# An expert layer that adds its weighted rows by accumulating scatters, with four shared tiles behind the routed ones

## Chip, cores and metric

One core of one Trainium2 chip runs the kernel. The metric is device time in microseconds (us), the median of several runs. The profile is of one more execution of the program, recorded by the hardware profiler.

## What is computed

Eight sequences of 512 tokens by 512 features go through attention with rotary embedding, then through a second block: RMS norm, latent attention with a residual, RMS norm again and a mixture of experts, whose result is normalized and added to the first attention's output. The change lies in the mixture. Each token gets the shared expert and its two best of seven routed experts, weighted by their scores:

```python
shared = expert_ffn(x, sh_gate, sh_up, sh_down)
probs = jax.nn.sigmoid(x @ router_w + router_b)
scores, idx = jax.lax.top_k(probs, TOPK)            # TOPK = 2
scores = scores / jnp.sum(scores, axis=-1, keepdims=True)
w = jnp.sum(jax.nn.one_hot(idx, NR) * scores[..., None], axis=-2)   # NR = 7
for e in range(NR):
    combined = combined + w[..., e:e + 1] * expert_ffn(x, r_gate[e], r_up[e], r_down[e])
return shared + combined
```

with `expert_ffn(x, wg, wu, wd) = (silu(x @ wg) * (x @ wu) / 8) @ wd` and a hidden width of 256. The kernel adds the block's own input `h` to this sum, applies a layer norm to the result, and adds the first attention's output `x1`. That is its output.

## The kernel before, in words

`attention_layers` makes, sequence by sequence, `x1` and `h` and stores them in HBM (`store_h`, L465 to L469), with an order of steps written by a planner. Beside it ScalarE's queue clears the slots for routed rows with `clear` (L678).

`expert_layer` (L1103) works in units of 512 tokens, which `unit(u)` walks through on each engine. Units 0 to 7 are the eight sequences with the shared expert's weights; units 8 to 29 are 22 tiles of routed rows, with the weights of one routed expert each, read from a table. A unit on TensorE (L1923) is four products of 12 matmuls into the ring `into` (gate and up for two halves of the hidden width, banks for gate and up in turn) and two down products of 12 into `down`. Each float32 product is three matmuls of rounded high and low parts. ScalarE takes the tanh and the high parts, VectorE the gating and the low parts (`gate`, `full_acts`, `low_acts`). Weights are loaded by SyncE (SP) into `raw` and split into `wh` and `wl` (`split`).

Between the products stands the opening of a later unit: four columns of transposes (`transposed_rows`) whose high and low parts go to `xh` and `xl`, and for a sequence also its squares, scale and norm (`squares`, `row_scale`, `normed`), its logits, their transposes, the choice of two experts (`routing`), a rank count on TensorE (`rank`, L1909: one product and ten of 7 columns) and the slot numbers (`placing`). Unit u opens sequence u + 2 and places sequence u + 1; two openings come ahead of unit 0. All these use the two banks of the ring `opening` in turn. Then GpSimd scatters the normed rows of the sequence to their two slots in HBM, eight indirect DMAs of 128 rows (`scatter`, L1416). SP loads sequence s into the place of sequence s - 4 in `xr` only when that one is scattered (`load_x`, L1275). When all eight are placed, `make_table` gives the experts and places of the 22 tiles, and SP loads the tiles from the slots (`load_rows`).

The shared result is added to `h` in `hsum` by VectorE (`add_shared`) and stored as `summed`. The routed results are copied to `y` by ScalarE (`take_y`) and stored as `y_slots`. Behind the last unit comes a loop over the eight sequences: SP loads `x1` and `summed` (`load_back`), GpSimd gathers both rows of each token by the numbers that `answers` made (`bring`, L1425: eight indirect DMAs), VectorE adds them weighted by `share` (`gather_rows`), takes statistics, and after `close_scale` on GpSimd normalizes and adds `x1` (`close`), and SP stores. Two sequences are in hand at a time:

```python
for s in range(blocks):
    store(s)
    if s + 2 < blocks:
        load_back(s + 2)
```

Every engine runs its own list in order, and semaphores tie the lists together.

## Time and profile before

| | us |
|---|---|
| median of 3 runs | 2620.97 (2616.71 to 2624.66) |
| profiled execution | 2623.76 |
| its span | 2622.0 |
| busy: TensorE | 2222.6 (85%) |
| VectorE | 1542.5 (59%) |
| ScalarE | 1043.9 (40%) |
| GpSimd | 991.2 (38%) |

In the rows below, PE is TensorE (PEld its weight loads), DVE VectorE, ACT ScalarE, POOL GpSimd and SP SyncE; a q behind a name is that engine's queue, which issues DMAs and waits. PEclk is TensorE's granted clock as a share of the full one, DMA the busy share of the core's 16 DMA engines. Times are from the span's start. L1868 is the line of the helper that issues nearly all products, so groups are told apart by the tiles that they write and read.

### The profile page before, as it was taken

The numbers are of one execution on the slowest core, as the hardware profiler recorded it, in microseconds if no ns is written. First come the engines' busy times: TensorE is split into PE (matmuls) and PEld (weight loads), VectorE is DVE, ScalarE is ACT, GpSimd is POOL, SyncE is SP. The second block draws the span as 40 slices with busy tenths as digits, with TensorE's granted clock in tenths as the row PEclk, the third lists the DMA queues.
The fourth block names the chain that finished last, engine by engine and source line by source line (L and its number), as shares of the span: only waits on it lengthen the run. The fifth ranks groups of instructions, "written<-read, shape, count | busy, mean of one in ns | idle before, by whom it ended". The sixth has DMA issues, their size and how long they took to land. (4 is left out here: it accounts for less than half of the span.)

```text
span 2622.0 us, 38025 instructions
## 1 busy us (share of the span) xinstructions
PE 2222.6 (85%) x12992; PEld 1523.9 (58%) x12992; DVE 1542.5 (59%) x4168; ACT 1043.9 (40%) x2164; POOL 991.2 (38%) x1049
## 2 busy tenths in 40 slices
PE   6898888999888999988899989895899899999700
PEld 5665555665555566554565655552677688888500
DVE  3656656656566565656656566663555555565377
ACT  1335443334444333445433444542332355555300
POOL 1445544435454344536343454542343000000174
PEclk9999989999999999999999999996899899999955
DMA  5334454444445354353553434443354555555397
GB/s 174 97 97 128 123 160 123 113 115 120 129 119 148 109 142 113 98 153 97 155 144 100 131 101 116 109 115 124 127 213 164 209 199 195 207 187 212 145 325 255
DMA packets 228430, 386.11 MB, mean 147 GB/s; under 512 B 24718, under 2 KB 108558, under 8 KB 222606
## 3 DMA queue, kind: packets, MB, share of 16 engines
q1 hardware_dynamic: 157710, 290.87, 37.2%
q10 hardware_dynamic: 60288, 59.25, 7.0%
q0 software_dynamic: 10240, 33.56, 3.5%
q8 instruction: 105, 1.72, 0.3%
q14 instruction: 87, 0.71, 0.1%
HBM read 141.90 MB, written 140.51 MB: 108 GB/s over the span
## 5 line engine op out<-in xcount | busy, mean ns | idle before, releaser
L819 DVE CUSTOM_DVE_ANT_0 unused<-score,mask 128x128 bf16<-128x128 f32 (+3 forms) x1024 | 467.8, 486 | 337.9 <-PE score L1000 324.9
L638 ACT ACTIVATE probs<-scoresT 128x512 f32<-128x512 f32 (+3 forms) x1024 | 418.2, 436 | 610.3 <-PE scoresT L1023 606.3
L1000 PE MATMUL score<-stacks 96*128 96x256 f32 (+2 forms) x1024 | 394.9, 429 | 96.8 <-DMA stacks<-parts 61.7
L1023 PE MATMUL scoresT<-stacks 97*128 97x256 f32 (+2 forms) x1024 | 408.8, 434 | 17.8 <-ACT probs L638 10.7
L571 POOL TENSOR_TENSOR probs<-probs 128x1536 f32<-128x1536 f32 (+1 forms) x128 | 373.8, 2920 | 52.4 <-PE out_ps L1037 45.7
L1000 PEld LDWEIGHTS score<-stacks 96*128 96x128 f32 x1024 | 183.1, 195 | 308.7 <-issue 183.5
L560 POOL TENSOR_SCALAR_AFFINE_SELECT probs<-probs 128x512 f32<-128x512 f32 x256 | 164.3, 642 | 349.4 <-ACT probs L638 349.2
L832 DVE RECIPROCAL total<-total 128x128 f32<-128x128 f32 x256 | 232.6, 932 | 94.9 <-ACT whole L649 89.5
L930 PE MATMUL middle<-wqkv,XT 128*128 128x128 f32 x2048 | 270.1, 280 | 7.0 <-ACT XT L605 6.1
L930 PEld LDWEIGHTS middle<-wqkv,XT 128*128 128x128 f32 x2048 | 260.4, 195 | 21.9 <-issue 8.4
L1058 PE MATMUL middle<-wo,outT 128*128 128x512 f32 x512 | 261.5, 606 | 0.0
L1023 PEld LDWEIGHTS scoresT<-stacks 97*128 97x128 f32 x1024 | 190.2, 195 | 117.3 <-ACT probs L638 68.5
L1431 POOL DMA_INDIRECT wh<-y_slots,answer x32 | 48.3, 1511 | 450.0 <-DMA y_slots<-y 441.2
L1037 PE MATMUL out_ps<-probs,V 128*32 128x512 f32 (+3 forms) x2048 | 205.0, 474 | 4.2 <-POOL probs L560 3.7
L1868 PE MATMUL into<-xh,wh 128*128 128x512 f32 x480 | 198.2, 413 | 0.0
L1868 PE MATMUL into<-xl,wh 128*128 128x512 f32 x480 | 190.2, 396 | 0.0
L1868 PE MATMUL into<-xh,wl 128*128 128x512 f32 x480 | 190.2, 396 | 0.0
L550 POOL TENSOR_TENSOR qk<-qk,turned 128x512 f32<-128x512 f32 x64 | 81.3, 1270 | 270.2 <-DVE turned L763 270.2
L759 DVE TENSOR_TENSOR qk<-middle,rope 128x512 f32<-128x512 f32 (+1 forms) x128 | 70.8, 553 | 126.8 <-PE middle L930 80.6
L1748 DVE SCALAR_TENSOR_TENSOR acts<-acts,into 128x512 f32<-128x512 f32 x60 | 41.2, 687 | 168.0 <-ACT acts L1514 166.0
L801 DVE TENSOR_TENSOR parts<-middle,parts 128x512 fp32r<-128x512 f32 x128 | 84.9, 685 | 80.0 <-ACT parts L614 78.0
L981 PE MATMUL middle<-wqkv,XT 128*128 128x512 f32 x256 | 129.2, 597 | 0.0
(174 smaller groups left out, 3732.6 us busy)
## 6 DMA issues: line engine op xcount, KB each, us to landing
stacks<-parts SPq DMA_DIRECT2D x768, 128.0 KB, 2.8
x_slots<-mask ACTq DMA_DIRECT2D x56, 1024.0 KB, 6.8
xr<-x_slots SPq DMA_DIRECT2D x22, 1024.0 KB, 6.1
y_slots<-y SPq DMA_DIRECT2D x22, 1024.0 KB, 4.3
raw<-in_gates SPq DMA_DIRECT2D x23, 512.0 KB, 3.9
raw<-in_ups SPq DMA_DIRECT2D x23, 512.0 KB, 4.9
raw<-in_downs SPq DMA_DIRECT2D x23, 512.0 KB, 5.7
normed<-in_L_attn_x SPq DMA_DIRECT2D x8, 1024.0 KB, 7.9
```

The lines of the kernel that those rows point to most:

```text
L560: pool.affine_select(out=diagonal, in_=diagonal, compare_op=ALU.is_ge, fill=0.0, base=0, pattern=[[0, GH], [1, P]], channel_multiplier=-1)\
L571: pool.tensor_tensor(probs[0][:, :, P * j:T], probs[0][:, :, P * j:T], probs[j][:, :, :], ALU.add)\
L638: act.activation(probs[j][:, h, 0:width], scoresT[:, u % ST_BANKS, first:first + width], ACT.Exp, scale=SCALE).then_inc(exp_done, 1)
L819: ins = dve.tensor_tensor_reduce(unused[:, t, 0:width], score.bank(name)[:, first:first + width], mask[:, T - width:T], 1.0, MASKED, ALU.a ...
L832: dve.reciprocal(total[:, mine], total[:, mine]).then_inc(inverted, 1)
L930: ins = pe.matmul(to, tile_of(xT, c, t), wqkv[:, c, first:first + P], start=(c == 0), stop=(c == CT - 1))
L981: ins = pe.matmul(middle.bank(name), tile_of(xT, c, t), wqkv[:, c, 2 * D:3 * D], start=(c == 0), stop=(c == CT - 1))
L1000: ins = pe.matmul(score.bank(name)[:, first:first + width], heads[0:ROWMAX, 0, h, t * P:(t + 1) * P], heads[0:ROWMAX, 1, h, 0:width], star ...
L1023: pe.matmul(scoresT[:, u % ST_BANKS, 0:T - first], heads[0:ROWMAX + 1, 1, h, j * P:(j + 1) * P], heads[0:ROWMAX + 1, 0, h, first:T], start ...
L1037: ins = pe.matmul(out_ps[h * HD:(h + 1) * HD, P * j:T], v[:, c % 2, j, head:head + HD], probs[j][:, h, :], start=(j == 0), stop=(j == TT - 1))
L1058: ins = pe.matmul(middle.bank(name), tile_of(outT, (NG * f + c) % OUTS, t), wo[:, core_of(f)[1], c, :], start=(c == 0), stop=(c == CT - 1))
L1868: ins = pe.matmul(to, left, right, start=(first and n == 0), stop=(last and n == len(pairs) - 1))
```

## The change

The expert layer is written anew around one list of steps, `expert_order`, from which every engine takes its own.

- There are 30 units as before: four shared sequences (0 to 3, "early"), the 22 routed tiles, and the four other shared sequences (4 to 7, "late").
- All eight sequences are opened in the first three units, in the order 0, 4, 1, 5, 2, 6, 7, 3. Only sequence 0's columns come ahead of unit 0. The late ones' normed rows are stored (`normed_kept`) and loaded and transposed again for their units.
- A row scattered to a slot carries four numbers more (`ROW = D + 4`): the smaller share, the difference of the shares, the first expert and the token's number. From them `goals` makes each routed tile's weights (`gain`) and target rows (`goal`). ScalarE applies the weight when it copies the down product out.
- `summed` gets the early sequences with their shared result and the late ones as plain `h`, stored by the attention layers. GpSimd adds each routed tile to it by four accumulating indirect DMAs (`give`). Each waits for the landing of the one before, since two additions to a row at once would lose one. Rows of empty slots go to rows that nobody reads.
- Gone are `y_slots`, `answers`, the gathers (`bring`) and `gather_rows`.
- The closings (`close_stats`, `close_scale`, `close_norm` on ScalarE now, `close`) stand in the order 4, 0, 5, 1, 6, 2, 7, 3: two each in the last three late units, one ahead of the down products and one behind them, and two behind the last unit. A late sequence's closing adds its down product. The loads of `summed` (`load_sums`) wait for the last three tiles' additions.
- `rank` counts with one product of 35 columns and four of 28, 21, 14 and 7.

The core of the diff:

```diff
+                    if s >= EARLY:
+                        sp.dma_start(summed[s * T:(s + 1) * T, :].rearrange("(t p) c -> p t c", p=P), rows[:, :, :])\
+                          .then_inc(h_stored, 16)
...
-                    CLEAR = T - 2 * P
+                    CLEAR = TT * ROW // 6
...
+ROW = D + 4
+EARLY = 4
+GIVEN = 3
+SUMS = 2 + GIVEN
...
+                def rows_free(o):
+
+                    b = o - XR
+                    if b >= 0:
+                        sp.wait_ge(*opening.full(("xT", b, CT - 1)))
+                    if 0 <= b < blocks:
+                        sp.wait_ge(scattered[b], 16 * TOP * TT)
+                        if sequences[b] >= EARLY:
+                            sp.wait_ge(xn_kept[sequences[b] - EARLY], 16)
+                    if blocks <= b < blocks + routed:
+                        sp.wait_ge(goal_done, b - blocks + 1)
...
+                def give(k):
+
+                    if k == 0:
+                        pool.wait_ge(h_kept, 16 * EARLY)
+                    pool.wait_ge(goal_done, k + 1)
+                    for t in range(TT):
+
+                        if t > 0:
+                            pool.wait_ge(y_given[k % GIVEN], 16 * (TT * (k // GIVEN) + t))
+                        elif k > 0:
+                            pool.wait_ge(*given(k - 1))
+                        pool.wait_ge(y_done, TT * k + t + 1)
+                        pool.indirect_dma_start(
+                            out=summed, out_offset=bass.IndirectOffsetOnAxis(ap=goal[:, k % XR, t:t + 1], axis=0),
+                            in_=y[:, k % GIVEN, t, :], in_offset=None, compute_op=ALU.add).then_inc(y_given[k % GIVEN], 16)
...
+                def load_sums(m):
+                    s = closing[m]
+                    if m == 0:
+                        sp.wait_ge(h_kept, 16 * EARLY)
+                        for k in range(routed - GIVEN, routed):
+                            sp.wait_ge(*given(k))
+                    if m >= SUMS:
+                        sp.wait_ge(out_ready, TT * (m - SUMS + 1))
...
+                def goals(k):
+
+                    beside = xr[:, (blocks + k) % XR, :, D:ROW]
+                    dve.wait_ge(x_in[(blocks + k) % XR], 16 * ((blocks + k) // XR + 1))
+                    if k >= XR:
+                        dve.wait_ge(*given(k - XR))
+                    if k > 0:
+                        dve.wait_ge(goal_done, k)
+                    dve.scalar_tensor_tensor(out=gain[:, k % XR, :], in0=beside[:, :, 2], scalar=expert[:, k:k + 1],
+                                             in1=beside[:, :, 1], op0=ALU.is_equal, op1=ALU.mult).then_inc(goal_step, 1)
...
+                        if m == 0 and u > 0:
+                            pe.wait_ge(*evacuated(u - 1, t))
...
+        if late > 0:
+            yield from closing_of(2 * late - 2)
+        yield "DN", u, 0
+        yield "DN", u, 1
+        if late > 0:
+            yield from closing_of(2 * late - 1)
+    for m in range(2 * (blocks - EARLY) - 2, blocks):
+        yield from closing_of(m)
```

How the lists change at three places. In these rows a name ahead of `<-` is what the instruction writes, and what stands in brackets is the semaphores that it waits for.

First, VectorE between the gate and up products of unit 0 and its end. L1589 (L1816 in the changed kernel) are squares of a sequence, L1644 (L1877) begins the placing of one, and L1606 (L1836) the routing of one. Before, unit 0's end:

```order
L1748 SCALAR_TENSOR_TENSOR acts<-acts,into 128x512 [waits tanh_done]
L1595 SCALAR_TENSOR_TENSOR xl<-opening,ln2w,xh 128x512 [waits x_high]
L1755 SCALAR_TENSOR_TENSOR acts<-acts,into 128x512 [waits into_filled,into_freed0]
L1761 TENSOR_TENSOR actl<-acts,acth 128x512 [waits act_high]
L1595 SCALAR_TENSOR_TENSOR xl<-opening,ln2w,xh 128x512 [waits x_high]
L1644 TENSOR_TENSOR place<-opening,offset 128x28 [waits opening_filled]
```

and in the changed kernel:

```order
L1980 TENSOR_TENSOR actl<-acts,acth 128x512 [waits act_high]
L1823 SCALAR_TENSOR_TENSOR xl<-opening,ln2w,xh 128x512 [waits x_high]
L1816 ISA junk,square<-xr 128x512 [waits squared,padded2_done,x_in0]
L1816 ISA square 128x1
L1816 ISA junk,square<-xr 128x512
L1816 ISA square 128x1
L1816 ISA junk,square<-xr 128x512
L1816 ISA square 128x1
L1816 ISA junk,square<-xr 128x512
L1816 ISA square 128x1
L1877 TENSOR_TENSOR place<-opening,offset 128x28 [waits opening_filled]
```

The squares of the fifth opened sequence, which wait for its load into the first one's place (`x_in0`), now stand ahead of the placing of the second, and behind that the routing of the third.

Second, GpSimd from the last sequences to the routed tiles. Before, the last two scatters and the first gathers:

```order
L1421 DMA x_slots<-xr,slot 28672x512 [waits placed]
L1421 DMA x_slots<-xr,slot 28672x512 x7
L1421 DMA x_slots<-xr,slot 28672x512 [waits placed]
L1421 DMA x_slots<-xr,slot 28672x512 x7
L1431 DMA wh<-y_slots,answer 128x512 [waits y_kept1,y_kept0,answered]
L1431 DMA wh<-y_slots,answer 128x512 x3
```

and in the changed kernel:

```order
L1639 DMA x_slots<-xr,slot 28672x516 [waits placed]
L1639 DMA x_slots<-xr,slot 28672x516 x7
L1655 DMA h_summed<-y,goal 4224x512 [waits y_done,goal_done,h_kept]
L1655 DMA h_summed<-y,goal 4224x512 [waits y_done,y_given0] x3
L1655 DMA h_summed<-y,goal 4224x512 [waits y_done,y_given0,goal_done]
L1655 DMA h_summed<-y,goal 4224x512 [waits y_done,y_given1] x3
```

The gathers are gone, and each of the four additions of a tile waits for the one before (`y_given`).

Third, VectorE and a sequence's closing. Before, one turn of the last loop:

```order
L1817 SCALAR_TENSOR_TENSOR hsum<-wh,share,hsum 128x512 [waits back_in0_0,h_in0]
L1817 SCALAR_TENSOR_TENSOR hsum<-wh,share,hsum 128x512 x3
L1817 SCALAR_TENSOR_TENSOR hsum<-wl,share,hsum 128x512 [waits gained,back_in0_1]
L1817 SCALAR_TENSOR_TENSOR hsum<-wl,share,hsum 128x512 [waits gained] x3
L1824 BN_STATS stats<-hsum 128x6 [waits gained] x4
L1827 BN_AGGR meanvar<-stats 128x2 [waits stats2_done] x4
L1833 TENSOR_SCALAR hsum<-hsum,meanvar,rstd 128x512 [waits rstd2_done]
L1833 TENSOR_SCALAR hsum<-hsum,meanvar,rstd 128x512 x3
L1838 TENSOR_TENSOR y<-hsum,y 128x512 [waits closed,x1_in0]
L1838 TENSOR_TENSOR y<-hsum,y 128x512 [waits closed] x3
```

and in the changed kernel, the third late unit from its last low part on:

```order
L1823 SCALAR_TENSOR_TENSOR xl<-opening,ln2w,xh 128x512 [waits x_high]
L1999 TENSOR_TENSOR y<-down,y 128x512 [waits down_filled,back_in2]
L1999 TENSOR_TENSOR y<-down,y 128x512 [waits down_filled] x3
L2006 BN_STATS stats<-y 128x6 [waits meanvar2_done,late_added] x4
L2011 BN_AGGR meanvar<-stats 128x2 [waits shift2_done,stats2_done] x4
L2018 TENSOR_TENSOR xr<-hsum,xr 128x512 [waits closed,x1_in1]
L2018 TENSOR_TENSOR xr<-hsum,xr 128x512 [waits closed] x3
L2006 BN_STATS stats<-y 128x6 [waits meanvar2_done,back_in3]
L2006 BN_STATS stats<-y 128x6 [waits meanvar2_done] x3
L2011 BN_AGGR meanvar<-stats 128x2 [waits shift2_done,stats2_done] x4
L2018 TENSOR_TENSOR xr<-y,xr 128x512 [waits closed,x1_in2]
L2018 TENSOR_TENSOR xr<-y,xr 128x512 [waits closed] x3
```

Two closings stand between the gating of one late unit and that of the next. The weighted adds of gathered rows and the normalization are no longer on VectorE.

## Rows read from the trace of the kernel before

**Rows 1.** Busy time of each engine by stage; columns as in the first row, in us.

```profile
core 0: us, PE busy (x) PEld busy (x) DVE busy (x) ACT busy (x) POOL busy (x), PEclk, DMA share, GB/s
0.00:1814.00 1814.00, 1602.76 (x10048) 1030.83 (x10048) 1088.88 (x3202) 744.74 (x1649) 824.59 (x874) 0.96 0.43 121
1814.00:1862.00 48.00, 20.70 (x87) 12.13 (x87) 19.11 (x59) 17.58 (x31) 6.17 (x21) 0.59 0.47 165
1862.00:2073.00 211.00, 198.05 (x964) 155.00 (x964) 113.50 (x358) 60.30 (x103) 69.36 (x74) 0.94 0.55 195
2073.00:2474.00 401.00, 401.00 (x1897) 325.94 (x1896) 222.03 (x358) 220.68 (x382) 0.00 (x0) 1.00 0.52 186
2474.00:2622.00 148.00, 0.07 (x1) 0.00 (x0) 98.95 (x192) 0.60 (x2) 91.07 (x80) 0.51 0.82 291
```

**Rows 2.** Chain of waits, 2474 to 2622 (start, duration, what).

```profile
2520.85 6.37 DMA out<-y
...
2527.64 11.10 DMA hsum<-h_summed
```

**Rows 3.** Chain of waits, routed stage: the down products of two tiles in a row.

```profile
2303.44 5.59 PE down L1868 x24
...
2321.97 5.59 PE down L1868 x24
```

**Rows 4.** Timeline, shared stage: a rank count; the first tanh of two units in a row.

```profile
1875.36 2.48 PE L1919 MATMUL opening<-either,ones 128*128 128x7 f32 x20
...
1941.46 0.60 ACT L1514 ACTIVATE acts<-into 128x512 f32<-128x512 f32 x1
...
1965.90 0.60 ACT L1514 ACTIVATE acts<-into 128x512 f32<-128x512 f32 x1
```

**Rows 5.** Who waited for whom, TensorE, 1862 to 2475.

```profile
PE opening L1885 <- DMA xr<-x_slots: 12.8, 1, 12.8
```

**Rows 6.** DMA issues: queue, count, size, median us to landing.

```profile
xr<-h_kept SPq DMA_DIRECT2D x8, 1024.0 KB, 6.3
...
out<-y SPq DMA_DIRECT2D x8, 1024.0 KB, 5.0
...
x_slots<-xr,slot POOLq DMA_INDIRECT x64, 2.7
```

**Rows 7.** Timeline, start of the expert layer.

```profile
1814.84 0.38 SPq L1281 DMA_DIRECT2D xr<-h_kept  x1
...
1835.23 0.59 PE L1868 MATMUL opening<-xh,wrh 128*7 128x512 f32 x1 [1.77 <-DVE xl L1595]
...
1842.58 3.70 DVE L1579 TENSOR_TENSOR wl<-raw,wh 128x512 fp32r<-128x512 f32 x6 [5.17 <-ACT wh L1470]
...
1861.98 0.48 PE L1868 MATMUL into<-xh,wh 128*128 128x512 f32 x1
```

**Rows 8.** Busy time in the last 17.3 us of the shared stage, behind the hole.

```profile
2050.90:2068.20 17.30, 17.30 (x75) 13.89 (x74) 11.84 (x19) 7.40 (x13) 0.00 (x0) 0.88 0.33 113
```

**Rows 9.** Timeline, last sequence: slot numbers, last scatter's issue, load of the first tiles.

```profile
2027.87 0.17 DVE L1664 CAST slot<-slotf 128x8 uint32<-128x8 f32 x1
...
2037.22 0.96 POOL L1421 DMA_INDIRECT x_slots<-xr,slot  x1 [0.30 <-issue]
...
2044.84 1.51 SPq L1310 DMA_DIRECT2D xr<-x_slots  x2
```

**Rows 10.** DMA issues, 2028 to 2045.

```profile
x_slots<-xr,slot POOLq DMA_INDIRECT x8, 6.1
```

**Rows 11.** Groups of instructions, 1862 to 2474 (count, busy us, mean ns, idle before).

```profile
L1768 DVE TENSOR_TENSOR hsum<-down,hsum 128x512 f32<-128x512 f32 x32 | 21.6, 691 | 40.0 <-PE down L1868 39.8
```

**Rows 12.** Groups of instructions, 2474 to 2622.

```profile
L1838 DVE TENSOR_TENSOR y<-hsum,y 128x512 f32<-128x512 f32 x32 | 19.9, 683 | 0.0
...
L1824 DVE BATCH_NORM_STATS2 stats<-hsum 128x6 f32<-128x512 f32 x32 | 19.7, 679 | 0.0
...
L1442 POOL TENSOR_TENSOR rstd<-padded,minus_half 128x4 f32<-128x4 f32 x8 | 8.3, 1044 | 0.7
```

More of the change, by code:

```diff
@@ new lines, in _ @@
+                for step, *which in order:
+                    if step == "LX":
+                        load_x(*which)
+                    if step == "LS":
+                        load_small()
+                    if step == "LW":
+                        load_weights(*which)
+                    if step == "LH":
+                        load_h(*which)
+                    if step == "LR":
+                        load_tile(blocks + which[0])
+                    if step == "XT" and which[1] == CT - 1 and which[0] < blocks and sequences[which[0]] >= EARLY:
+                        keep_normed(which[0])
+                    if step == "OUT" and units.kinds[which[0]][0] == "early":
+                        keep_h(units.kinds[which[0]][1])
+                    if step == "LSM":
+                        load_sums(*which)
+                    if step == "LX1":
+                        load_x1(*which)
+                    if step == "ST":
+                        store(*which)
@@ L1376, in _ @@
+                for n in range(XR):
+                    sp.wait_ge(stored[n], 16 * (blocks // XR))
             @block.gpsimd
@@ L1446, in _ @@
[L1446 to L1461 removed]
+                                out=flat_slots, out_offset=bass.IndirectOffsetOnAxis(ap=slot[:, o, j, t:t + 1], axis=0),
@@ L1463, in _ @@
+                pool.wait_ge(consts, N_POOL)
+                for step, *which in order:
+                    if step == "SQ":
+                        row_scale(*which)
+                    if step == "RK":
+                        scatter(*which)
+                    if step == "OUT" and units.kinds[which[0]][0] == "routed":
+                        give(units.kinds[which[0]][1])
+                    if step == "CA":
+                        close_scale(*which)
             @block.scalar
@@ L1466, in split @@
                 def split(i, k):
+                    if k == 0:
+                        act.wait_ge(raw_in, 48 * (i + 1))
+                    if k == 0 and i >= 2:
+                        last = max(u for u in range(len(units)) if units.weights(u) == i - 2)
+                        act.wait_ge(*down.full((last, TT - 1)))
                     n, half_of = divmod(k, 2)
@@ new lines, in columns_free @@
+                def columns_free(o):
+                    u = units.unit_of.get(o)
+                    if u is not None and u >= 2:
+                        act.wait_ge(*into.full(("up", u - 2, FT - 1)))
+                        if u - 2 < EARLY:
+                            act.wait_ge(*opening.full(("z", units.opening[u - 2])))
+                    if u is None:
+                        earlier = [b for b in range(o) if b not in units.unit_of]
+                        if earlier:
+                            act.wait_ge(*opening.full(("z", earlier[-1])))
@@ L1963, in _ @@
-                pe.wait_ge(consts, N_POOL)
-                for s in range(2):
-                    for c in range(CT):
-                        transposed_rows(s, c)
-                    logits(s)
-                    logits_by_token(s)
-                rank(0)
-                for u in range(units):
-                    unit(u)
+                        pe.wait_ge(*opening.out(("xT", o, CT - 1)))
+                        pe.wait_ge(*opening.out(("xT", o, CT - 2)))
+                    name = ("gate", "up")[n], u, m
@@ new lines, in into_hidden, with out_of_hidden @@
+                    pairs = []
+                    for c in range(CT):
+                        first = c * FF + m * P
+                        pairs += three((wh, xh), (wl, xl), np.s_[:, i % 2, n, first:first + P],
+                                       np.s_[:, units.home(o), c, :])
+                    pe.wait_ge(*into.empty(name))
+                    product(into.bank(name), pairs).then_inc(into.filled, 1)
+                def out_of_hidden(u, m):
+                    i = units.weights(u)
+                    pe.wait_ge(act_low, u * FT + m + 1)
+                    for t in range(TT):
+                        if m == 0 and u > 0:
+                            pe.wait_ge(*evacuated(u - 1, t))
+                        ins = product(down.bank((u, t)),
+                                      three((acth, wh), (actl, wl), np.s_[:, m, t * P:(t + 1) * P],
+                                            np.s_[:, i % 2, 2, m * D:(m + 1) * D]),
+                                      first=(m == 0), last=(m == FT - 1))
+                        if m == FT - 1:
+                            ins.then_inc(down.filled, 1)
@@ new lines, in _ @@
+                pe.wait_ge(consts, N_POOL)
+                for step, *which in order:
+                    if step == "XT":
+                        transposed_rows(*which)
+                    if step == "LG":
+                        logits(*which)
+                    if step == "ZT":
+                        logits_by_token(*which)
+                    if step == "RK":
+                        rank(*which)
+                    if step == "GU":
+                        into_hidden(*which)
+                    if step == "DN":
+                        out_of_hidden(*which)
```

901 lines of the change are left out of this document (465 added, 436 removed).

## Prediction

> **What bounds the kernel now.** I read the busy time by stage first [rows 1]. The attention layers take 1814 us, and the change touches them only at two edges. The expert layer then has four stages: 48 us before the first gate product, 211 us with TensorE busy for 198 (the eight shared tiles, with routing beside them), 401 us with TensorE busy for all of it at clock 1.00 (21 of the 22 routed tiles), and 148 us in which TensorE does nothing. Next the chain of waits of that last stage [rows 2]: it runs through loads of a summed sequence, 11.1 us each, and stores of 6.4 us. Eight sequences are fetched back, gathered, normalized and stored by VectorE and the DMA engines alone. In the routed stage the chain is TensorE without a break: 18.53 us from one tile's down products to the next one's [rows 3]. In the shared stage a unit takes 24.4 us [rows 4], since it also opens one sequence. There is one hole in it: 12.8 us [rows 5], in which the first routed tile is awaited. So the idle 148 us is the prize, and whatever the change puts into the first two stages or behind the routed ones is its price.
>
> The sum is made against the profiled execution: span 2622.0 us and time 2623.76, while the median of the runs is 2620.97. It therefore ends with +1.8 for what lies around the span and -2.8 to the median, together -1.
>
> **Edge of the layers: +2.7.** Four sequences are stored twice, the last two stores of 1 MB together at the end of the layer, where nothing hides them. 1 MB is 3.6 us at the last stage's mean of 291 GB/s [rows 1], and less where nothing else moves; the bounds are 0 (they overlap) and 5 (a whole out store [rows 6]). I take 2.7. The other three lie beside 50 us of attention without a wait for them. The cleared slots grow by 1/128, hidden in the same way.
>
> **Start of the expert layer: -21.5.** Before, both openings (with logits) come ahead of the first product: 47.1 us from the first load to it [rows 7]. Now only sequence 0's columns do. They are in at 1835.2; then VectorE has the next sequence's squares (2.5) and six weight splits (3.7), so the products start near 1840.5. Bounds -18 and -23.
>
> **The early units: -34.** Before, eight shared units take 206.2 us, from the first gate product [rows 7] to 2068.2, where the first routed tile's begins [rows 8]. Now four units carry all eight openings. TensorE's work: a unit's four gate and up products and its down product are 18.53 less 1.4 for four columns of transposes, 17.1; an opening is 1.4 of columns, 2.8 of logits, 0.35 of their transposes and a rank count, which falls from 20 small passes (2.5 us [rows 4]) to 8, about 1.25 with the product ahead of it. 4 x 17.1 + 8 x 1.4 + 8 x 4.4 is 115. I then followed the queues. Three things stop TensorE:
> - A slot of rows is loaded anew only when its sequence has been scattered. From the slot numbers to the last of eight scatters' issue are 9.3 us [rows 9], then 2.7 to landing and 6.3 for the load [rows 6]: 18 us. VectorE asks for those rows with some 14 us of work in between, and waits before the placing and routing on which TensorE's next ranks and zT transposes hang. That is 4 to 6 us in each of units 0 to 2.
> - Logits, tanh, routing and rank of one sequence now follow each other with one product between instead of a unit, and use two banks in turn: 2 to 5 us in each unit more. By my walk units 0 to 2 take 42, 34 and 45, of which 23 is waiting.
> - Three sequences are opened in unit 2. The last two scatters run one behind the other: 16 x 1.26 = 20 us of issue instead of 10, and landings beside the weight load. Before, 16.9 us go by from the last slot numbers to the load [rows 9]; now about 21 from the last ones. The hole grows from 12.8 to 21.
> 115 + 23 + 21 is 159, plus some 13 for TensorE at its lower clock after such stops (the granted clock was 0.94 in this stage [rows 1], 0.88 after the hole [rows 8]): 172. Minus 206 is -34. Bounds: with half the waits -55; with twice those of units 0 to 2 -10.
>
> **The routed units: 0, with one unknown.** The answer table, the y stores and the 64 gathers go. Four tiny goal operations per tile on VectorE, which is busy 222 of 401 us, are free. The new work is the accumulating scatter: four per tile on GpSimd, each waiting for the landing of the one before. No row shows one. Below, it is bounded by the plain scatter in a quiet fabric, 2.7 us from issue to landing [rows 6]; above, by the same scatter beside a weight load and a store, 6.1 [rows 10]. It must read what it adds to, but runs alone in its queue, and only the weight and row loads (2.5 MB, some 7 of 18.5 us) meet it; so I take 4.3, nearer the quiet row. A tile then costs 4 x 4.4 = 17.6 us, under 18.53: hidden. The cover is thin. If a tile costs G, the last addition ends 22 x G behind the first one's start, which is 21 units (389 us) ahead of the first late unit. The loads of summed rows, which wait for it, can start some 27 us into that unit and still be in when VectorE asks for them in the second. So the penalty is 22 x G - 415 us where positive; it starts at 4.6 us an addition with 0.1 between.
>
> By the Trainium skill, Collectives: The Full Stack, section "The bandwidth ceiling: the fold count and why AG ≠ RS ≠ AR", an add in the DMA engines is slow "because the add needs **two source reads**", and moves at half the rate of a copy. If only the data's part of a scatter doubled (an estimated 0.7 us, a quarter MB at nearly 400 GB/s), an addition would be an estimated 3.4 us and the sum would stay as it is; if the rule held for the whole time, it is the second rival.
>
> **The late units: +88.8.** Four shared units come behind the routed ones: the first undisturbed, 18.5. From the second on VectorE has per unit its own 7 us, and two closings: one add of the down product (4 x 0.69 [rows 11]), two statistics (4 x 0.61), aggregates, two additions of the attention's output (4 x 0.63 [rows 12]): 13.4. That is 20.4 against TensorE's 18.5, and the next unit's tanh stands on ScalarE behind both normalizations, whose scales GpSimd makes in about 2 us (1.04 for the power [rows 12]). TensorE waits for the gate bank and for the add. My walk gives 21.7, 23.5 and 25.1.
>
> **The end: -119.** Before, 147.9 us from the last product to the end. Now five of the eight closings are behind VectorE or in its hands when the last product ends; left are the final addition of one and two whole closings, 5.6 + 2.5 + 2.9 + 2.5 in a row, 2 + 2.6 for the last scales and normalization, the last additions and a store of 5.0 [rows 6]: 29.
>
> **The sum:** 2.7 - 21.5 - 34 + 88.8 - 119 = -83. 2622 - 83 = 2539; I add 6 for additions that now and then miss the cover, and with -1 the median is about **2545**.
>
> **Rivals.**
> - *The early units lose little*: the loads are in on time and banks free early. For it, the shared stage now has only its one hole. Against it, the 18 us of scatter and reload, each part of which has a row. It gives 2545 - 22 = 2523.
> - *An addition takes twice a plain scatter in all*: 5.4 and 0.1 between, G = 22, penalty 69. For it, the added read of the target; against it, that a quiet scatter's 2.7 is largely not data. 2539 + 69 - 1 = 2607. A middle case at 5.0 (G 20.4, penalty 34) gives 2572.
> - *The additions become the bound, and it ends slower*: each takes 6.1 as in [rows 10], G = 24.8, penalty 131, 2669. It decides from 5.6 us an addition (G = 22.7). For it, the weight and row loads that share the fabric; against it, that those eight scatters were issued back to back and queued among themselves, while here one at a time is under way.
> - *The change does not overlap what it says*: the closings wait for the last addition in any case, and then only VectorE's order counts; a tail of 60 instead of 29 would give 2576. It falls into the middle case.
>
> **How the numbers follow.** The forecast has 0.50, the first rival 0.08, the middle case 0.20, doubled additions 0.07, the slower one 0.12, and 0.03 is for a result near no change. The range runs from 2508 to 2605: it holds the forecast, the first rival and most of the middle case, and leaves out the bound additions and half of the doubled ones. A measurement of this kernel tells 0.3% (8 us) from no change. Faster by more: 0.50 + 0.08 + 0.20 + 0.06 = 0.84. Within: 0.03. Slower: 0.13.
>
> **What would show it.** The time from the first expert load to the first gate product near 26 us; units 0 to 2 over 30 us each, with VectorE waiting for a load of rows ahead of a placing; one wait for the first routed tile near 21 us; routed units still at 18.53 with GpSimd waiting for an addition's landing most of the time, 4 to 4.7 us from issue to landing; late units of 21 to 25 us; under 35 us behind the last product. I am wrong if the routed units are longer than 18.6, if GpSimd is still adding when the second late unit starts, or if the early units take over 195 us.

## The result: 2.2% slower, the additions became the bound

| | us |
|---|---|
| before, median of 4 runs | 2619.8 (2616.7 to 2624.7) |
| changed, median of 4 runs | 2679.4 (2673.5 to 2683.3) |
| ratio | 1.022, 95% interval 1.0197 to 1.0246 |
| forecast | 2545 (2508 to 2605) |

The forecast was wrong in sign and size. The result lies near the slower rival's 2669. The profiled execution has a span of 2671.3 us, 49.3 over that of before.

The busy time of each engine by stage, cut at the changed kernel's own borders; it answers to [rows 1]. The stages are attention; the start of the expert layer; four shared units; 22 routed units; four late units; the end:

```profile
core 0: us, PE busy (x) PEld busy (x) DVE busy (x) ACT busy (x) POOL busy (x), PEclk, DMA share, GB/s
0.00:1809.00 1809.00, 1601.14 (x10048) 1031.04 (x10048) 1089.63 (x3202) 746.16 (x1649) 824.60 (x874) 0.96 0.44 124
1809.00:1835.00 26.00, 4.07 (x17) 3.16 (x18) 12.00 (x28) 10.23 (x18) 5.82 (x22) 0.50 0.86 304
1835.00:2013.00 178.00, 132.37 (x625) 97.46 (x626) 94.85 (x382) 53.99 (x96) 70.95 (x76) 0.87 0.54 193
2013.00:2508.00 495.00, 434.69 (x1938) 349.61 (x1937) 241.58 (x438) 225.43 (x392) 119.74 (x75) 0.94 0.61 163
2508.00:2641.00 133.00, 83.19 (x336) 65.70 (x335) 52.48 (x100) 31.15 (x49) 31.76 (x33) 0.79 0.61 169
2641.00:2671.00 30.00, 0.45 (x2) 0.01 (x1) 23.06 (x48) 11.22 (x16) 10.65 (x12) 0.55 0.60 210
```

The routed stage had TensorE busy without a break before. Now it is 495 us long for 435 us of products, and the late units take 133 us for 83. Who waited for whom there: first TensorE and ScalarE in the routed stage (2013 to 2508), then TensorE in the late units (2510 to 2642). Columns: who, for what, us in total, times, longest.

```profile
PE into L2060 <- DVE acts L1967: 56.6, 13, 6.9
PE into L2060 <- DVE acts L1974: 3.7, 1, 3.7
...
ACT y L1751 <- DMA h_summed<-y,goal: 144.5, 13, 13.7
...
PE down L2060 <- DVE hsum L1999: 36.2, 1, 36.2
```

ScalarE scales a tile's down product into one of three `y` buffers. From the ninth tile on it waits 10 to 14 us for the additions of the tile three before, and the next unit's first tanh is queued behind it. TensorE then waits for VectorE's gating, which waits for that tanh. So TensorE's rows name VectorE, though what holds everything up is on GpSimd.

GpSimd's timeline shows the cause. These are the additions of one tile in the middle and the first of the next (start, duration, idle before and what ended it), then the last four:

```profile
2243.01 1.55 POOL L1655 DMA_INDIRECT h_summed<-y,goal  x1 [6.39 <-ACT y L1751]
2247.91 1.92 POOL L1655 DMA_INDIRECT h_summed<-y,goal  x1 [3.35 <-DMA h_summed<-y,goal]
2253.65 1.97 POOL L1655 DMA_INDIRECT h_summed<-y,goal  x1 [3.82 <-DMA h_summed<-y,goal]
2260.84 1.55 POOL L1655 DMA_INDIRECT h_summed<-y,goal  x1 [5.23 <-DMA h_summed<-y,goal]
2267.76 1.55 POOL L1655 DMA_INDIRECT h_summed<-y,goal  x1 [5.37 <-ACT y L1751]
...
2556.99 1.55 POOL L1655 DMA_INDIRECT h_summed<-y,goal  x1 [4.10 <-issue]
2561.87 1.55 POOL L1655 DMA_INDIRECT h_summed<-y,goal  x1 [3.33 <-DMA h_summed<-y,goal]
2566.98 1.57 POOL L1655 DMA_INDIRECT h_summed<-y,goal  x1 [3.56 <-DMA h_summed<-y,goal]
2571.95 1.56 POOL L1655 DMA_INDIRECT h_summed<-y,goal  x1 [3.40 <-DMA h_summed<-y,goal]
```

A tile takes 24.8 us (2243.01 to 2267.76). Over all, the first addition started at 2036.6 and the 88th at 2571.95: 535.4 / 87 = 6.15 us each. The wait of one hangs on the landing of the one before nearly everywhere. The two rows that name ScalarE's `y` are no exception: each is the first addition of a tile, whose own `y` had been written some 50 us earlier. The write that ended there is that of the tile two further on, which the same landing had set free. The last addition was issued 64 us into the late units, and the chain of waits goes on from there:

```profile
2566.98 4.70 DMA h_summed<-y,goal
2571.68 0.27 issue
2571.95 4.82 DMA h_summed<-y,goal
2576.76 0.02 issue
...
2576.85 5.44 DMA hsum<-h_summed
2582.29 0.02 issue
2582.32 2.48 DVE hsum L1999 x4
```

The first summed rows are in at 2582.3, and VectorE adds the first late unit's down product to them. TensorE needed those banks for the second late unit's down products, 36.2 us earlier.

The stages against the forecast, in us. Borders are the issue of the last store of `h_kept`, the first load behind it, the first gate product, the first routed product, the end of the last routed product, the end of the last product, the end of the span:

| stage | before | after | change | forecast |
|---|---|---|---|---|
| attention | 1810.1 | 1801.9 | -8.2 | 0 |
| edge | 4.8 | 7.5 | +2.7 | +2.7 |
| start of the expert layer | 47.1 | 25.5 | -21.6 | -21.5 |
| shared units ahead | 206.0 | 178.1 | -27.9 | -34 |
| routed units | 406.1 | 495.2 | +89.1 | 0 (+6 for missed cover) |
| late units | 0 | 133.4 | +133.4 | +88.8 |
| end | 147.9 | 29.9 | -118.0 | -119 |

Whether the -8.2 in attention is an effect of the change is not shown. In the 13 executions of the changed kernel and its variants below, which share that code, the same store is issued between 1797.9 and 1808.7, so most of it is spread. All 13 lie below the 1810.1 of before, but of that kernel there is one profile.

### The profile page after: what moved, and what is told of

Its sections match the earlier page's. It is cut to its first block and busy times, and to the rows that moved or that the text cites. A ratio compares the mean times of both kernels' runs of the same rounds, so it can differ in the third digit from the quotient of the medians.

```text
span 2671.3 us, 38251 instructions
## 1 busy us (share of the span) xinstructions
PE 2255.9 (84%) x12960; PEld 1547.0 (58%) x12960; DVE 1513.6 (57%) x4196; ACT 1078.2 (40%) x2218; POOL 1063.5 (40%) x1092
## 5 line engine op out<-in xcount | busy, mean ns | idle before, releaser
L1031 PE MATMUL scoresT<-stacks 97*128 97x256 f32 (+2 forms) x1024 | 407.9, 434 | 19.8 <-ACT probs L646 10.3
L1655 POOL DMA_INDIRECT h_summed<-y,goal x88 | 140.3, 1594 | 448.3 <-DMA h_summed<-y,goal 268.0
L2060 PE MATMUL into<-xh,wh 128*128 128x512 f32 x480 | 213.0, 444 | 75.5 <-DVE acts L1967 64.1
L2060 PE MATMUL into<-xl,wh 128*128 128x512 f32 x480 | 202.6, 422 | 0.0
L2060 PE MATMUL into<-xh,wl 128*128 128x512 f32 x480 | 202.3, 421 | 0.0
L2060 PEld LDWEIGHTS into<-xh,wh 128*128 128x128 f32 x480 | 98.9, 206 | 100.1 <-DVE acts L1967 68.1
L2060 PE MATMUL down<-wh,acth 128*128 128x512 f32 x240 | 100.5, 419 | 42.3 <-DVE hsum L1999 36.2
## 6 DMA issues: line engine op xcount, KB each, us to landing
stacks<-parts SPq DMA_DIRECT2D x768, 128.0 KB, 2.8
```

The costliest lines, as they stand in the source:

```text
L1031: pe.matmul(scoresT[:, u % ST_BANKS, 0:T - first], heads[0:ROWMAX + 1, 1, h, j * P:(j + 1) * P], heads[0:ROWMAX + 1, 0, h, first:T], start ...
L1655: pool.indirect_dma_start(out=summed, out_offset=bass.IndirectOffsetOnAxis(ap=goal[:, k % XR, t:t + 1], axis=0), in_=y[:, k % GIVEN, t, :] ...
L2060: ins = pe.matmul(to, left, right, start=(first and n == 0), stop=(last and n == len(pairs) - 1))
```

## Experiments

Times of before differ by up to 10 us from one set of runs to another (medians 2619.8 to 2630.3), so kernels are compared by their ratio to the runs of before in their own set.

**Four additions in flight.** A tile holds slots of one expert, so no token stands in it twice, and its four additions need not wait for each other. Only the rows for empty slots had to be made distinct among the four:

```diff
-                        if t > 0:
-                            pool.wait_ge(y_given[k % GIVEN], 16 * (TT * (k // GIVEN) + t))
-                        elif k > 0:
+                        if t == 0 and k > 0:
                             pool.wait_ge(*given(k - 1))
-        nobody = sb("nobody", [P, 1])
+        nobody = sb("nobody", [P, TT])
```

> The four additions of a tile are issued one behind the other, each tile still waits for the landings of the one before it (a tile holds one expert, so no token is twice in it; padding rows get a row of their own for each of the four). In the changed kernel 88 additions took 6.15 us each, one at a time, 24.6 us a tile against 18.53 of TensorE's work. Theory A (it is the round trip, waited for 88 times, that bounds): four overlap, a tile costs 4 x 1.55 of issue + about 4 of landing = 10 us, is hidden, the routed stage goes back from 495 to 406 us and the 36 us wait in the first late unit goes: 2679 - 89 - 36 = about 2554. Theory B (the accumulation itself is slow in the queue, each needs its 4 us of the queue alone): a tile still costs over 18 us, and the time stays above 2620. Theory C (weight and row loads slow them): they are in flight together with the loads just the same, and a tile costs 4 x 4 = 16 to 20 us, time 2555 to 2620.

Measured: 2559.3 against 2626.4, ratio 0.975 (0.9723 to 0.9775), where theory A had about 2554. The additions of one tile, and the first of the next:

```profile
2197.08 1.55 POOL L1653 DMA_INDIRECT h_summed<-y,goal  x1 [11.16 <-ACT y L1749]
2198.93 1.55 POOL L1653 DMA_INDIRECT h_summed<-y,goal  x1 [0.30 <-issue]
2200.79 1.55 POOL L1653 DMA_INDIRECT h_summed<-y,goal  x1 [0.31 <-issue]
2202.65 1.79 POOL L1653 DMA_INDIRECT h_summed<-y,goal  x1 [0.30 <-issue]
2215.62 1.55 POOL L1653 DMA_INDIRECT h_summed<-y,goal  x1 [11.17 <-ACT y L1749]
```

and its routed, late and last stages:

```profile
2025.00:2438.00 413.00, 409.40 (x1937) 332.84 (x1936) 239.60 (x438) 234.27 (x395) 135.71 (x84) 1.00 0.78 202
2438.00:2531.00 93.00, 80.65 (x339) 64.03 (x337) 52.44 (x100) 30.07 (x47) 17.51 (x24) 0.91 0.65 212
2531.00:2561.00 30.00, 0.38 (x2) 0.00 (x0) 22.73 (x48) 11.20 (x16) 7.88 (x12) 0.55 0.58 211
```

GpSimd now waits for `y`, not for landings. The routed stage has its clock of 1.00 and no stop but one of 3.6 us, and the 36.2 us wait in the second late unit is gone. The additions waiting for each other are shown as the cause. The distinct rows for empty slots are not what did it: the kernel with three trips, below, has them too and stays slow.

**What of a round trip is the addition?** The same kernel as changed, but the scatters write (`compute_op` left out):

> The scatters of weighted rows write instead of adding (the sums are left out); every wait is kept. Theory A: what is paid is the round trip, so a plain write costs over 5 us a piece as well, at most 0.5 us less than the addition's 6.15, and the time falls by under 60 us, to 2620 to 2679. Theory B: the read of the target is what costs; a write takes the 3 to 4 us of the plain scatters of rows, a tile under 18.5, and the time falls to about 2550.

Measured: 2563.2, one run. Duration on GpSimd (least, median, most) and landing, for the write and then for the addition:

```profile
L1655 POOL DMA_INDIRECT h_summed<-y,goal x88: 957/964/1476, 2047.8 to 2452.1; - x88
...
DMA to landing us min/median/max: 2.7/3.3/8.5
```

```profile
L1655 POOL DMA_INDIRECT h_summed<-y,goal x88: 1550/1550/2063, 2036.6 to 2571.9; - x88
...
DMA to landing us min/median/max: 4.4/5.0/10.3
```

So here theory A, as I had put it, failed: a write in the same chain costs far less than 5 us. By the medians adding costs 1.7 us more from issue to landing, and the 0.6 us more on GpSimd are a part of them. Both the adding and the chain are needed for the loss: a chain of writes was hidden, additions four at a time are hidden too, and only additions in a chain are not.

**No additions at all**, to see what the rest gives:

> No weighted rows go out at all (GpSimd only signals, the output lacks the routed experts). It shows what everything but the additions gives. All theories: 2679 - 89 - 36 = about 2550, with routed units of 18.5 us; my sum without its 6 us for missed cover was 2538. If the late units still take over 95 us for four without a wait for summed rows, that term was wrong by itself.

Measured: 2555.6, one run, 4 us from the kernel with four in flight, whose own runs lie 7 us apart. Its late units take 93.1 us, those with four in flight 93.0. So additions in flight cost nothing that can be seen, and the late term was 4 us short by itself. The routed units take 413.4 us in both, 7.3 more than before, so these 7.3 are not the additions' doing. Some 5.5 of them lie in the first routed unit: it takes 24.0 us where before's took 18.5, with the stop of 3.6 us in it and a clock of 0.93.

**Less traffic beside the additions:**

> From the second routed tile on only a third of each expert's weight bytes is loaded (512 KB instead of 1.5 MB, the rest stays from the tile before, so the output is another); the additions and all waits stay. In the changed kernel additions come every 6.15 us while weights are loaded and every 5.1 us in the last twelve, behind the last load. Theory C (contention makes the difference): every 5.3 us or less, 21.2 us a tile, time 2679 - 88 x 0.85 = about 2604. Theory A with a price that does not depend on the loads: 6.1 us, no change from 2679.

Measured: 2648.6, one run, between what the two theories gave (2604 and 2679). One addition every 5.81 us in place of 6.15. The last twelve of the changed kernel, with no weight load near, came every 5.1. So two thirds of the weight bytes account for about 0.34 us of the 1.05 that traffic adds to an addition; whether the tile's own load of 1 MB is the rest was not tried.

**Three trips a tile instead of four:**

```diff
-                        if t > 0:
+                        if t > 1:
                             pool.wait_ge(y_given[k % GIVEN], 16 * (TT * (k // GIVEN) + t))
-                        elif k > 0:
+                        elif t == 0 and k > 0:
```

> Between the changed kernel and the one with four additions in flight: the second addition of a tile is issued right behind the first, the third and fourth still wait for the landings before them. Three round trips a tile instead of four: G = 3 x 6.15 + 1.85 = 20.3 us, penalty 22 x 20.3 - 415 = 32 us on the 2559 of four in flight: 2591 (the mechanism: nothing is lost until a tile's additions take longer than a routed unit, and then 22 times the excess). Rival, that the additions are only bound when all are serial, or that the two in flight slow each other by as much as they save: 2559, or 2650 and more.

Measured: 2635.2 against 2630.3, ratio 1.002 (0.9991 to 1.0048). My 2591 was wrong, and the timeline says where. Two tiles' starts, one among loads and the last one:

```profile
2214.03 1.96 POOL L1655 DMA_INDIRECT h_summed<-y,goal  x1 [3.89 <-issue]
2216.30 1.55 POOL L1655 DMA_INDIRECT h_summed<-y,goal  x1 [0.30 <-issue]
2225.07 1.55 POOL L1655 DMA_INDIRECT h_summed<-y,goal  x1 [7.21 <-DMA h_summed<-y,goal]
...
2523.39 1.55 POOL L1655 DMA_INDIRECT h_summed<-y,goal  x1 [3.84 <-issue]
2525.24 1.55 POOL L1655 DMA_INDIRECT h_summed<-y,goal  x1 [0.30 <-issue]
2530.70 1.57 POOL L1655 DMA_INDIRECT h_summed<-y,goal  x1 [3.90 <-DMA h_summed<-y,goal]
```

A pair takes 7.3 us in the quiet case where I had allowed 8.0. Of the 22 pairs, 17 took 7.1 to 8.0, one 8.7, and four 10.3 to 11.2, as the first one shown. So the surplus of a loaded tile is not spread evenly over its trips. In the middle of the changed kernel (tiles 9 to 19) the last two carry it: from the start of the first, second, third and fourth addition to the next one it is 5.1, 5.3, 7.2 and 7.3 us on average. Four trips took 24.8 us among loads and 20.4 in quiet (4 x 5.1), three trips 22.4 and 17.7. The surplus is 4 to 5 us a tile either way. What I took away was a trip of the quiet price: it saved 2.4 to 2.7 us a tile, and not the 4.3 that I had counted (24.6 less 20.3).

With the tile times that the traces show, the forecast's penalty, 22 x G - 415, can be tested. G is the distance of the first addition of the last tile from that of the first, over 21. The loss is the time less that of four in flight, scaled to the same runs of before (0.975 of them):

| kernel | G | 22 x G - 415 | measured loss |
|---|---|---|---|
| changed | 24.8 | 131 | 125 |
| less weight traffic | 23.4 | 99 | 89 |
| three trips | 22.4 | 77 | 71 |
| four in flight | 18.5, TensorE's own pace | 0 | 0, by definition |

The mechanism and its threshold were right, within 10 us, for G between 22.4 and 24.8; the size of G was not.

**The early units.** Two reorderings of the kernel with four in flight. First, the first routed tile's columns behind the fourth shared unit's down products, where TensorE had stood still in the middle of that unit:

```diff
+        if u == EARLY - 1:
+            first = None
...
         if u == EARLY - 1:
+            yield from [("XT", blocks, c) for c in range(CT)]
             yield "EX", 0
```

> With four additions in flight, and the columns of the first routed tile are opened behind the down products of the fourth shared unit instead of inside its gate products, where TensorE waited 16.6 us for that tile's load (span 2561.5). The unit's remaining 17 us of products then run during the wait. Expected: the wait falls to about 0 to 3, and what is exposed instead is the chain columns, high and low halves of the first tile, some 5 us: 2559 - 10 = about 2549. If the wait is not on the path (VectorE or the weight splits are late instead), no change: 2559.

Measured: 2555.8 in two runs 10 us apart, ratio 0.9715 (0.967 to 0.976), not to be told from 0.975. The wait for the load went, and two waits for VectorE's gating, 13.1 us together, came in its place. Then, VectorE's squares behind the placing:

```diff
-        yield from next(nexts, [])
+        then = next(nexts, [])
+        yield from then[:1]
         yield from routed_too("RK", first)
+        yield from then[1:]
```

> With four additions in flight, and in the early units VectorE's squares of the next sequence (which wait for its row load) stand behind the placing of the previous sequence instead of ahead of it, and so do GpSimd's scale and scatters. My theory of the early units: the wait for a reload ahead of a placing costs 4 to 6 us in each of units 0 to 2, together some 12 to 15 us: the time falls to about 2547. Rival: the chain logits, tanh, routing, rank is what stops TensorE there, not the placing; then at most 3 us are gained: 2556 to 2559.

Measured: 2546.8 against 2630.3, ratio 0.968 (0.9653 to 0.9709): some 18 us below 0.975 of its own runs of before, my 12 to 15 and a little more. VectorE's waits for a row load in this stage, first in the changed kernel, then here:

```profile
DVE junk L1816 <- DMA xr<-h_kept: 20.3, 4, 6.5
```

```profile
DVE junk L1816 <- DMA xr<-h_kept: 2.5, 2, 1.9
```

From the first gate product to the first weighted row went 193.0 us. Seven executions with the old order took 200.3 to 212.6 for it, and the first kernel below with six additions on GpSimd, whose early units are the same as here, took 190.1, so the wait ahead of the placing is shown as a cause there. That spread also says that 202.0 for the reordered columns shows nothing by itself.

**The late units.** ScalarE's second normalization behind the next unit's first tanh (a change of place in the list of steps), with four in flight:

> With four additions in flight, and ScalarE's second normalization of a late unit stands behind the next unit's first tanh instead of ahead of it. In the trace of four in flight ScalarE waits 7 to 9 us for the scales with the tanh queued behind, at four places. If that wait sets the late units (my walk's 21.7 to 25.1 us against 18.5 of products), up to 3 x 3 us go: about 2550. If VectorE's own work (closings of 13.4 plus 7 us) sets them, nothing changes: 2559.

Measured: 2557.2, two runs, ratio 0.972 (0.9688 to 0.9753), no difference that can be told. The trace says why: the late units came down from 93.0 to 86.9 us, and the end grew from 30.1 to 33.9, since VectorE there waited for a load of `x1` that is issued only when an earlier sequence is stored:

```profile
DVE xr L2021 <- DMA xr<-x_kept: 7.8, 1, 7.8
```

The same row has 4.1 us with four in flight. TensorE's waits in the late units with four in flight:

```profile
PE down L2059 <- DVE y L1998: 6.1, 2, 3.2
PE down L2059 <- DVE hsum L1998: 3.1, 1, 3.1
PE into L2059 <- DVE acts L1966: 3.1, 2, 2.4
```

With the later normalization the third row is gone. The first two stay, some 3.1 us in each of the last three late units: TensorE waits there for VectorE to add the down product of the unit before, and in every later kernel too. The other 3 us of the 6.1 are products at a higher clock: TensorE is busy 80.7 us at a granted clock of 0.91 with four in flight, and 77.5 us at 0.94 with the later normalization.

Then VectorE was relieved: six of the eight last additions on GpSimd, with the squares behind the placing, and next with the late columns as well:

> With four additions in flight and the squares behind the placing (2547), and the last addition of six of the eight closings (the attention's output plus the normalized layer, 2.5 us a sequence on VectorE) on GpSimd, which idles in the late units. If VectorE's queue sets the late units, as my walk said (7 + 13.4 = 20.4 us against 18.5 of products), its work falls to 15.4 a unit and the four late units fall from their 91 us to about 78, plus up to 3 at the end: about 2533. If it is ScalarE's waits or the round from statistics to scales that sets them, there is little to gain, since these stay: 2543 to 2549; and more than 2549 if GpSimd's slower additions (1.27 us against 0.69) delay the scales queued behind them.

> The one before, and also the first routed tile's columns behind the fourth shared unit's down products (which took 4 us by itself off the early stage, 202.0 from the first gate product to the first weighted row against 206.0). If the two are independent: 4 us below the one before, about 2529.

Measured: 2545.3 and 2540.8 against 2620.3, ratios 0.972 (0.9691 to 0.9751) and 0.970 (0.9671 to 0.9723). The late units stayed at 93.2 and 93.4 us, and the end grew to 35. VectorE's 5 us less work a unit showed no gain: it waited longer for the tanh instead (35.4 us, 9.6 at once, against 27.8 with four in flight). But these two kernels do not relieve VectorE alone, since GpSimd makes the scales as well. At the end of the third late unit, with six additions on GpSimd:

```profile
2477.81 0.37 DVE L2024 BATCH_NORM_AGGREGATE meanvar<-stats 128x2 f32<-128x6 f32 x4
...
2477.29 5.04 POOL L1684 TENSOR_TENSOR xr<-hsum,xr 128x512 f32<-128x512 f32 x4
2482.41 0.23 POOL L1664 TENSOR_SCALAR padded<-meanvar 128x4 f32<-128x4 f32 x1
```

The second closing's mean and variance were ready at 2478.2, and GpSimd began its scale 4.2 us later, right behind the first closing's additions; with four in flight it began 0.1 us after them. This is the rival of my own expectation, and at this place it took back what VectorE had gained. The late columns' 4 us between the two kernels (2545.3 and 2540.8) lie within their intervals; the way to the first weighted row went from 190.1 to 182.8 us with them here, but the two kernels after them, with the same early units, took 189.5.

> The last one (columns of the first routed tile late, squares late, six last additions on GpSimd) and ScalarE's second normalization behind the next tanh as well. With GpSimd's additions alone the four late units stayed at 93 us, with the later normalization alone they came to 87 and 4 of the 6 us were given back behind the last product, where VectorE waited 7.8 us for a load of the attention's output. If VectorE's queue and ScalarE's waits are two bounds of about the same size, only both together show the gain: late units of 78 to 82 us, and 2541 - 13 + 4 given back = about 2532 against 2541. If either alone was all there is to get: 87 us and 2537.

Measured: 2550.7 against 2629.0, ratio 0.970 (0.9679 to 0.9713). Late units of 86.9 us, as with the later normalization alone, and an end of 41. The 78 to 82 us of two bounds of one size did not come. What is shown is that the tanh behind ScalarE's wait for the scales costs 6 us of the late units. That VectorE's last additions cost nothing there is not shown, since all three kernels moved them to the engine that makes the scales.

From the last routed product to the end of the span took 123.1 us with four in flight, 120.8 with the later normalization, and 128.0 to 128.6 in the three kernels with GpSimd's additions (5.0 us a sequence there, 2.5 on VectorE). So the last kernel drops those:

> Four additions in flight, squares behind the placing, first routed tile's columns behind the fourth unit's products, second normalization behind the next tanh, and all last additions on VectorE again. From the last routed product to the end of the span it took 123 us with four in flight, 121 with the later normalization, 128 in all three kernels with GpSimd's additions: what a late unit gains there the tail gives back, since the closings and their loads of x1 form a chain of their own. So this one should be 7 us better than the one before it: 0.967 of before instead of 0.9696, some 2535 where before is 2622. If GpSimd's additions were not what lengthened the tail, it stays at 0.9696.

Measured: 2540.6 against 2627.4, ratio 0.967 (0.9644 to 0.969), the median of five runs. This one beats the changed kernel and, by 3.3%, the one before it. It keeps the whole change and takes three waits a tile out of it. The 121.4 us behind its last routed product are in line. Its ratio is where it was expected, but its interval overlaps with 0.9696, so that GpSimd's additions cost anything rests on the traces.

## Why the prediction was wrong, step by step

- **What bounds the kernel.** Right: the idle 148 us was there to be had. The end fell to 29.9 us (forecast 29). The terms written for the end add up to 25.6 only, with 2.5 for the last additions, so part of that agreement is luck.
- **Edge and start.** Right: +2.7 and -21.6.
- **Early units, -34.** Measured -27.9 (178.1 us against 172). By the first tanh of each unit they took 41.5, 43.6, 51.9 and 39.1; my walk, ahead of its 13 us for the clock, had 42, 34, 45. The hole came out at 18.7 us for 21. The mechanism, VectorE waiting for a row load ahead of a placing, is in the waits with 20.3 us and in the experiment that took it away. It was mis-sized, within its bounds, and this execution flatters it: by the same two borders the six others with the same early units took 183.8 to 190.5 us, some 6 to 12 more.
- **Routed units, 0. This is the step that failed: "so I take 4.3, nearer the quiet row".** I had a plain scatter's 2.7 below and 6.1 above, and took a value just under the middle of the two, with no row for what the adding costs. The least time of any addition was 4.4 us, the median 5.0. In the quiet end of the chain the landings took 4.4 to 5.0 us (median 4.7) and the additions came 5.1 apart, so some 0.4 us pass from a landing to the next issue, 0.27 in the chain shown above, where I had put 0.1. Loads added 1.05 on the mean. That makes 6.15 from one to the next against my 4.4, with the threshold at 4.7 (4.6 and 0.1 between), which itself was right. The stage took 89.1 us more; 7.3 of them are there without any addition, and my "6 for additions that now and then miss the cover" met that size by luck.
- **The rule on two source reads** (the Trainium skill, Collectives: The Full Stack, the section on the fold count, which states it of a ReduceScatter against an AllGather) would have made an estimated 5.4 of a plain scatter's quiet 2.7 if held for the whole time, and an estimated 3.4 for the data alone. The least landing was 1.6 times the write's (4.4 against 2.7) and the median 1.5 times (5.0 against 3.3), so the trace stands between the two.
- **The slower rival** had the bound right and nearly the time, 2669. Its price of 6.1 came near by luck. It was that of plain scatters issued back to back, and plain scatters one at a time beside the same loads took 3.3 us (median), which bears out my argument that those "queued among themselves". What makes 6.15 is the adding and the traffic together, and the rival's price had nothing for the adding. I gave it 0.12, as the chain's price hung on one assumed duration with no row of its own. With bounds of 2.7 and 6.1 around a threshold at 4.6 and no row between, that was far too little.
- **Late units, +88.8.** 93.0 us without the additions' delay: 4 short. I made VectorE's 20.4 us of work a unit the bound and had the tanh behind the normalizations beside it. The tanh is shown with 6 us, and TensorE's wait for VectorE's addition of the down product stands in the waits with 9.3. Whether the rest of VectorE's work costs anything is open. The other 40 us of the 133.4 are the 36.2 of the delayed sums and what followed, and belong to the step that failed.

What I could have read from the changed code, and did not: the wait between the additions of one tile is not needed. The Trainium skill, DMA: Bandwidth & Descriptors, section "Rules for kernel authors", asks for the earlier DMA's semaphore between an accumulating DMA and another access "of the same bytes", and the four of a tile touch different rows. Between tiles the wait stayed in every kernel here, and no run shows what happens without it.

## What to carry to other kernels

A chain of small transfers, each waiting for the one before, is priced by its whole period, from issue to landing to the next issue, and times the number of links. Where an estimate without a row of its own stands close to a threshold, the chance belongs on both sides of it. Ask first which links touch the same rows: taking the needless waits away gave 4.7 percentage points here, more than all reordering behind it. And in a stage of several engines in a ring, like the late units, moving work from one engine to another tests the first only if the second is not in the ring too.

## What the runs showed of the hardware beyond that

- An accumulating scatter of 128 rows of 2 KB holds GpSimd for 1.55 us where the writing one takes 0.96, and lands 1.7 us later (medians 5.0 and 3.3).
- Four in flight, issued 1.85 us apart beside weight and row loads, cost TensorE nothing; two overlapping in quiet took 7.3 us where two in a chain took 10.2.
- The same code took 1797.9 to 1808.7 us for the attention layers and 200.3 to 212.6 us for the early stage from one execution to the next, about as much as some of the effects studied. A difference under 10 us between the stage times of two single profiles told nothing here without the runs' medians beside it.
